# Spreading a batch's expert gates over the partitions in two transfers of four experts each, in place of four of two

## What is computed

```python
h = _layernorm(x) * (1 + ca) + sa
x = x + ga * _L0_attn_ref(h, ...)            # linear attention, 16 heads of 8
h = _layernorm(x) * (1 + cb) + sb
x = x + gb * _L0_ffn_ref(h, ...)
# _L0_ffn_ref, for every token: 8 experts, the best 2 count
probs = softmax(x2 @ router_w); top_p, top_e = top_k(probs, 2)
y = sum over the chosen e of top_p * (gelu(x2 @ w_in[e] + b_in[e]) @ w_out[e] + b_out[e])
```

## Time and profile before

| | |
|---|---|
| time, median of 3 runs | 372.89 us (371.85 to 373.71) |
| the profiled execution's own time | 372.75 us |
| its span, first to last instruction | 370.9 us |
| busy: PE, DVE, ACT, POOL | 354.1, 291.2, 306.5, 226.5 us |
| granted TensorE clock | 0.998 of full speed |
| all DMA | 47.84 MB, mean 129 GB/s |
| spreading the gates: 64 transfers of 512 KB | 5.0 us each from issue to landing (median) |

### The profile page before, as it was taken

The page is one execution under the profiler, slowest core; times in us unless marked ns, Lnnn a source line. Parts: engine busy times, 40 slices in busy tenths (PEclk is TensorE's granted clock), DMA queues, the critical chain, the costliest instruction groups (busy, mean ns, idle before and its releaser), DMA issues.

```text
span 370.9 us, 8258 instructions
## 1 busy us (share of the span) xinstructions
PE 354.1 (95%) x2532; PEld 321.6 (87%) x2532; DVE 291.2 (79%) x1063; ACT 306.5 (83%) x524; POOL 226.5 (61%) x220
## 2 busy tenths in 40 slices
PE   2987999999999999999999999999999999998996
PEld 1866879899999989999999989999999989997985
DVE  2799889987897967787897888888898978747653
ACT  3467899999999899899998999899977968885750
POOL 3255947595649666573838658494659856274551
PEclk9999999999999999999999999999999999999999
DMA  5155045352515262252707035350606051424481
GB/s 172 20 159 230 0 159 216 115 173 73 185 40 197 81 190 98 115 164 52 244 3 259 28 115 172 109 178 17 241 5 227 2 177 55 143 87 157 160 273 68
DMA packets 19106, 47.84 MB, mean 129 GB/s; under 512 B 2603, under 2 KB 6390, under 8 KB 18806
## 3 DMA queue, kind: packets, MB, share of 16 engines
q1 hardware_dynamic: 18432, 46.64, 37.7%
q10 hardware_dynamic: 630, 0.67, 0.6%
HBM read 42.82 MB, written 4.48 MB: 128 GB/s over the span
## 4 chain that ended last, share of the span: by engine, by line
PE 80%; DVE 7%; issue 6%; POOL 3%; ACT 2%; DMA 1%; ACTq 1%; DVEq 0%; POOLq 0%
PE pY L1052 27%; PE pH L1036 7%; PE pH L1038 7%; PE pH L1037 7%; PE pQV L1000 3%; PE pC L986 3%; PE pC L1007 3%; PE pB L1022 3%; PE pQV L978 2%; PE pQV L962 2%; PE pQV L964 2%; PE pQV L963 2%; PE pB L1014 2%; PE pA L941 2%; PE pC L994 2%
## 5 line engine op out<-in xcount | busy, mean ns | idle before, releaser
L1052 PE MATMUL pY<-wout,v 128*128 128x128 f32 x1024 | 130.7, 276 | 0.1
L1052 PEld LDWEIGHTS pY<-wout,v 128*128 128x128 f32 x1024 | 124.5, 192 | 4.6 <-DVE v L1516 0.8
L746 ACT ACTIVATE u<-pH,cols 128x512 f32<-128x512 f32 x128 | 85.3, 685 | 15.9 <-PE pH L1038 11.7
L427 POOL TENSOR_TENSOR v<-u,gate_bc 128x512 f32<-128x512 f32 x48 | 68.5, 1432 | 19.4 <-PE pY L1052 11.8
L1516 DVE TENSOR_TENSOR v<-u,gate_bc 128x512 f32<-128x512 f32 x80 | 62.0, 784 | 8.6 <-DMA gate_bc<-route_scratch 5.6
L1036 PE MATMUL pH<-h_hi,win_hi 128*128 128x512 f32 x128 | 59.0, 461 | 0.5 <-ACT u L746 0.5
L1037 PE MATMUL pH<-h_hi,win_lo 128*128 128x512 f32 x128 | 50.5, 395 | 0.0
L1038 PE MATMUL pH<-h_lo,win_hi 128*128 128x512 f32 x128 | 50.4, 394 | 0.0
L439 POOL TENSOR_TENSOR h_lo<-h,h_hi 128x512 fp32r<-128x512 f32 x16 | 20.3, 1272 | 36.0 <-ACT h_hi L674 36.0
L746 ACT ACT_TABLE_LOAD x27 | 34.6, 1283 | 0.5
L444 POOL TENSOR_TENSOR rstd<-ve,neg_half 128x4 f32<-128x4 f32 x16 | 18.7, 1168 | 23.9 <-DVE nm L1473 23.9
(11 more groups left out here) (156 smaller groups left out, 811.6 us busy)
## 6 DMA issues: line engine op xcount, KB each, us to landing
gate_bc<-route_scratch SPq DMA_DIRECT2D x64, 512.0 KB, 5.0
x_all<-in_L_attn_x SPq DMA_DIRECT2D x16, 256.0 KB, 5.0
out<-x_all SPq DMA_DIRECT2D x15, 256.0 KB, 2.6
gates<-gate_scratch SPq DMA_DIRECT2D x1, 1792.0 KB, 6.9
route_scratch<-gateT SPq DMA_DIRECT2D x64, 4.0 KB
gb_bc<-gb_scratch SPq DMA_DIRECT2D x1, 1024.0 KB, 7.9
win<-in_L_ffn_w_in SPq DMA_DIRECT2D x1, 512.0 KB, 5.6
wout<-in_L_ffn_w_out SPq DMA_DIRECT2D x1, 512.0 KB, 7.2
```

Of the source, the lines that this page charges most:

```text
L427: pool.tensor_tensor(v[:, e % U, :], u[:, e % U, :], gate_bc[:, b % 2, e, :], ALU.mult).then_inc(s["vp_done"], 1)
L746: act.activation(u[:, e % U, :], pH[:, e % 2, :], ACT.Gelu_apprx_tanh, bias=cols[:, e:e + 1]).then_inc(s["gelu_done"], 1)
L1052: i = mm(pY[:, t * P:(t + 1) * P], v[:, e % U, t * P:(t + 1) * P], wout[:, e, :], start=False, stop=(e == NE - 1), skip_group_check=True)
```

## The change

PARTS goes from 4 to 2. With it `spread_gates(n, j)` moves experts 0 to 3 for j = 0 and 4 to 7 for j = 1: 8 KB for each partition and 1024 KB in all, in place of 4 KB and 512 KB. `gates_here`, the waits in `store_gates` and the semaphores follow from PARTS. All calls with j = 2 and j = 3 are gone, and nothing else in SP's list is moved.

```diff
-    PARTS = 4
+    PARTS = 2
...
                 load_x(b + 5)
                 if b == -1:
                     spread_later_gates()
-                if has(b):
-                    spread_gates(b, 3)
                 store_gates(b + 1)
                 spread_gates(b + 1, 0)
                 spread_gates(b + 1, 1)
...
                 if b == -1:
                     spread_moe_gates()
-                spread_gates(b + 1, 2)
...
             for b in range(-1, 9):
                 step(b)
-            spread_gates(9, 3)
...
             store_gates(15)
             spread_gates(15, 0)
             spread_gates(15, 1)
-            spread_gates(15, 2)
             store_out(12)
             store_out(13)
-            spread_gates(15, 3)
             store_out(14)
             store_out(15)
```

More of the change, by code:

```diff
@@ L324, in _ @@
             spread_gates(10, 1)
-            spread_gates(10, 2)
-            spread_gates(10, 3)
             load_x(15)
@@ L330, in _ @@
             spread_gates(11, 1)
-            spread_gates(11, 2)
-            spread_gates(11, 3)
             store_gates(12)
@@ L335, in _ @@
             spread_gates(12, 1)
-            spread_gates(12, 2)
-            spread_gates(12, 3)
             store_gates(13)
@@ L340, in _ @@
             spread_gates(13, 1)
-            spread_gates(13, 2)
-            spread_gates(13, 3)
             store_gates(14)
@@ L346, in _ @@
             spread_gates(14, 1)
-            spread_gates(14, 2)
             store_out(10)
             store_out(11)
-            spread_gates(14, 3)
             store_gates(15)
```

## The result

The changed kernel takes 377.77 us in the median of 4 runs (377.16 to 378.14), the kernel before 372.97 beside it (371.85 to 373.71). The ratio is 1.0127, with a 95% interval of 1.0102 to 1.0153: 1.3% slower. The profiled execution took 377.45 us, 4.7 more than that of before. The forecast was 374.5 with a range to 377.0, so the time lies outside.

What follows compares the result with a forecast made beforehand. PE was taken to bound the kernel, busy 354.1 of 370.9 us. Delays of PE's own time, 0.45 + 0.4 + 0.45 + 0.25 + 0.25 = 1.8 us, on 372.75 gave 374.55, stated as 374.5; range 372.4 to 377.0.

Steps and rivals of the forecast that it cites:

- The first transfer lands 5.45 us after its issue, from the second of a pair: First 1024 KB of each batch, read from two 512 KB transfers: lands 5.45 us after issue, against 4.2 before, +1.25 us.
- A first landing below 4.7 us: Sign in the new profile that would show the forecast wrong; first landings at 5.3 to 6.2 us would show it right.
- The row of gb_bc: 128 x 2048 broadcast landing 7.9 us after issue behind two spreads; read as 1.2 to 1.5 us for each further 512 KB.
- The landing is the same in every batch: First transfer of any batch n: lands 5.45 us after issue, +1.25 us for experts 0 and 1.
- the bound of 6.2 us, from batch 15: Upper bound on the first landing: 6.2 us after issue, +2.1; used to price late landings in batches 14 and 15.
- 1. Batch 0, +0.45: DVE's weighing of expert 0, already waiting for the landing, ends 1.25 us later and delays PE's combine by 0.45 us.
- 2. Batch 7, +0.4: Late ve_o delays POOL's rstd_o and weighing of expert 1, then ACT's gelu and ekT; PE loses 0.4 us.
- 3. Batch 9, +0.45: 0.9 us of delay reach ve_o, for which POOL already waits; the exponential ends later and ek_back moves by 0.45 us.
- 4 and 5. Batches 14 and 15, +0.25 each: First weighing released later, just behind PE's combine: +0.1 us each, +0.95 and +0.9 with a late landing; 0.25 each taken.
- The middle batches, 0: Batches outside 0, 7, 9, 14 and 15: waits and slack behind the first weighing absorb the delay, so PE loses nothing.
- The earlier gates of experts 4 to 7, 0: These gates land earlier but cover waits of POOL or DVE, not PE: taken as 0, with 1 us kept for the range.
- The leak through DVE in the middle: Rival, 13 in 100: DVE doesn't absorb the delay; half a microsecond reaches expert 7 in seven batches, 3.5 more: 378 us.

Runs made afterwards that it cites:

- run 2: Changed kernel with each of its two waits fed by two transfers of 512 KB in place of one of 1024 KB: 381.46 us, 1.024 against the kernel before.
- run 3: Changed kernel with 16 small unused products at the start of PE's list: 375.52 us, 1.0082 against the kernel before.
- run 7: Changed kernel with 112 already satisfied semaphore waits at the start of PE's list: 374.65 us, 1.0038 against the kernel before.
- run 6: Kernel with two transfers in batches 0 and 7 alone and four in all other batches: 376.54 us, 1.0104 against the kernel before.
- run 12: Changed kernel with three swaps in POOL's list, around the weighing of expert 1 in three places: 374.79 us, 1.0039 against the kernel before.
- run 1: Changed kernel with PARTS 4 again, all four 512 KB transfers issued at once in the place of the two: 373.31 us, 1.0016 against the kernel before.
- run 10: Changed kernel with three transfers, of two, two and four experts, issued at once: 372.59 us, 0.9997 against the kernel before.
- run 11: Changed kernel with four transfers, of one, one, two and four experts, issued at once: 372.86 us, 1.0007 against the kernel before.
- run 8: Kernel before with 112 already satisfied semaphore waits at the start of PE's list, as a control: 373.32 us, 1.0015 against the kernel before.
- run 4: Kernel before with 16 small unused products at the start of PE's list, as a control: 375.38 us, 1.0066 against the kernel before.
- run 9: Changed kernel with 64 bytes of padding in gate_bc behind every two experts, so 1024 KB transfers have 4 KB rows: 378.05 us, 1.0132 against the kernel before.

## Why the prediction was wrong

**The first transfer lands 5.45 us after its issue, from the second of a pair.** This is the step that failed first. One transfer of twice the size landed at 4.6, half a microsecond later than one of 512 KB, while two transfers waited for together landed at 5.2 to 5.7 (run 2). The row of the pair measured two transfers in flight, and I took it for the price of bytes. A first landing below 4.7 us was my own sign of being wrong, and ten batches show one. The row of gb_bc had the same fault: it was issued behind two others.

**The landing is the same in every batch.** It isn't: 6.8 and 6.2 us in batches 0 and 7, where an instruction fetch takes one DMA engine for 1.6 and 2.1 us. That this is the cause, and not the place in the program, is shown by runs 3 and 7: both remove the late landings there, and in 7 the fetch and the late landing reappear together in batch 6 (6.6 us). It is the long fetches that do it: 1024 KB landed at 6.1 to 6.9 us with packets of 1.4 us and more, and at 5.3 and 5.5 with the two of 1.3 and 1.0 (runs 3 and 6). I had the bound of 6.2 us, from batch 15, but put it only on the tail.

**1. Batch 0, +0.45.** The mechanism was right and the size wrong: 1.8 us. The landing came 1.8 later and not 1.25, which gives 1.0 at the first combine by the prediction's own reckoning (0.8 of slack), and 1.0 it was. The gelu behind it made a second wait of 0.8, which the sum left out. How the second one splits between DVE and ACT is argued from the rows, not shown by a run.

**2. Batch 7, +0.4.** The chain was right, link by link, and run 12 shows it: with expert 1 weighed before rstd_O the loss in ek_back is gone at the same landing. Only the size was off: 1.6 us, and 0.3 just ahead of it, at a landing of +2.0. The weighing itself took 1.28 us, beside POOL's residual, where the row before has 0.69; ve_o made that up by taking 0.17 for 0.89.

**3. Batch 9, +0.45.** The chain was right and the size near: 0.6 in ek_back, and 0.2 some 10 us later. That is in part luck. The weighing of expert 0 and ve_o came 1.0 us later against PE's course, where I had reckoned 0.9, but the landing gave only 0.86 of it; the issue itself was 0.5 later against PE's course, which my sum didn't have, and 0.3 to 0.4 went into the slack. POOL's wait for ve_o there, 0.63 us before, in the changed kernel:

```profile
248.49 1.42 POOL L400 TENSOR_TENSOR rstd_o<-ve_o,neg_half 128x4 f32<-128x4 f32 x1 [1.73 <-DVE ve_o L1435]
```

**4 and 5. Batches 14 and 15, +0.25 each.** Measured: nothing. The landings moved by 0.5 and the combines had it to spare. The first weighings, which took 1.09 and 1.53 us before, took 0.69 and 1.14, so that a slower product had no part in it.

**The middle batches, 0.** Wrong in batch 4, where 0.4 us were lost. I had asked for each batch when DVE weighs expert 0 and had not asked what stands behind POOL's weighing of expert 1. In batch 4 this is the layer norm's rstd of a later batch. The changed kernel, POOL, then ACT:

```profile
138.10 1.29 POOL L411 TENSOR_TENSOR v<-u,gate_bc 128x512 f32<-128x512 f32 x1 [0.83 <-ACT u L730]
139.35 1.53 POOL L374 TENSOR_TENSOR rstd<-ve,neg_half 128x4 f32<-128x4 f32 x1
140.96 0.20 POOL L376 TENSOR_TENSOR nmr<-nm,rstd 128x4 f32<-128x4 f32 x1
...
141.20 1.65 ACT L672 ACTIVATE xn<-x_all,nmr,rstd 128x128 f32<-128x128 f32 x4 [0.96 <-POOL nmr L376]
```

The gates had landed at 138.0, 0.1 us before the weighing, which comes 0.7 later against PE's course than before; the gelu that the bracket names was over at 137.3. nmr and xn follow late, and ekT and ek_back stand behind xn. Run 12, which takes rstd first, has no loss there. Run 2 shows the rest: at a delay of some 1.4 us seven batches lose, three of which (4, 10 and 13) I had priced at zero.

**The earlier gates of experts 4 to 7, 0.** Right: runs 1, 10 and 11 move them without a gain. yg, which was to wait less, waits as long as before (22.1 us in all against 22.0).

**The rivals.** None was it. The leak through DVE in the middle gives the measured time, 378, but by a route that wasn't taken: the loss sits in four batches, two of them at a fetch. The two errors in my sum went opposite ways, a delay taken too large and a price for a delay taken too small. What stays between them is the fetch: 3.5 of 4.8 us by the pair of runs 7 and 8 (4.8 - 1.3), 4.7 by the pair of 3 and 4, whose intervals are wide, and 3.6 by run 6, which counts all that a transfer of 1024 KB costs in the two batches.

**Open.** Why one transfer of 1024 KB takes 4.6 us and two of 512 KB 5.4. Why the fetch costs a transfer of 1024 KB nearly its whole 2 us and one of 512 KB less. How long its packet takes goes with it: first transfers of 512 KB landed at 4.2 with packets of 0.95 and 1.15 us, at 4.4 to 4.9 with 1.35 to 1.45, and mostly at 4.9 to 5.3 with 1.6 to 2.0. But the packet's own length may come from the data that it shares the engine with, and no run separated the two. And why the same delay costs PE different amounts: batch 7 cost 3.5 us in the profiled execution of run 9, at a landing of 6.1, and 1.9 in that of the changed kernel, at 6.2.

## What to carry to other kernels

When an engine is busy 95% of the time, merging transfers is judged by the landing of the first part that someone waits for, in each batch by itself: keep what is needed first in a small transfer of its own (run 10), and merge the rest. Before a delay is priced, follow every engine's queue behind the instruction that waits, and not only the one that waits first; a delay of some 1.4 us, priced at 1.8 us in all, cost 8.5. And what a change costs can hang on where instruction fetches fall: when a difference sits in one or two batches, move PE's list by a few harmless instructions in both kernels before a cause is named.

## What the runs showed of the hardware that I had not expected

- An instruction fetch of 16 KB goes through the same DMA engines as the data, and its packet takes one of 16 for 0.9 to 2.5 us (336 of them in sixteen traces). A transfer of 1024 KB that one of 1.4 us or more fell into landed at 6.1 to 6.9 us and not at 4.6, since its last engine decides.
- The fetches move with the length of PE's list: 112 waits that were already satisfied moved one from batch 7 to batch 6, and made the changed kernel 3.1 us faster.
- From issue to landing, in the batches without a fetch, before and after the change: 512 KB 3.8 to 4.3 us, 1024 KB 4.1 to 4.8 in one transfer. In the runs: 256 KB 3.1 to 3.5, and 1024 KB in two transfers 5.2 to 5.7. Rows of 4 or 8 KB make no difference.
